# Two more batches turned by VectorE, and the stores of a cross-attention kernel put off

## The reference, cut to what matters

```python
rgb, geo = transpose(x), transpose(g)          # (16, 1024, 128)
def heads(x, w): return (x @ w.T).reshape(b, n, H, d).transpose(0, 2, 1, 3)
def xca(q, k, v):
    attn = softmax(einsum('bhni,bhnj->bhij', q, k) * scale, axis=-1)
    return merge_heads(einsum('bhnd,bhde->bhne', v, attn))
res_p2r = xca(heads(rgb, wq_rgb), heads(geo, wk_point), heads(geo, wv_point)) @ proj_p2r.T
res_r2p = xca(heads(geo, wq_point), heads(rgb, wk_rgb), heads(rgb, wv_rgb)) @ proj_r2p.T
return transpose(rgb + res_p2r) + transpose(geo + res_r2p)
```

## Time and profile before

| | |
|---|---|
| median of 3 runs | 129.18 us (129.02 to 129.22) |
| the profiled execution's own time | 129.13 us |
| its span, first to last instruction | 127.1 us |
| busy: TensorE (PE), VectorE (DVE), ScalarE (ACT), GpSimd (POOL) | 120.8, 71.4, 86.4, 77.3 us |
| DMA moved | 34.25 MB, 25.69 MB read from HBM and 8.39 MB written |
| DMA queue of SP (q1), of ScalarE (q10) | 29.36 MB, 4.72 MB |
| the chain that ended last | PE 84%, DMA 5%, ACT 3% |

### The profile page before, as it was taken

One profiled execution on the slowest core, in us unless ns is written; L12 is line 12 of the kernel. 1 busy time (PEld: TensorE's weight loads), 2 busy tenths in 40 slices (PEclk: granted clock), 3 DMA queues, 4 the chain that ended last, 5 costly groups with the idle time before them and its releaser, 6 DMA issues.

```text
span 127.1 us, 2678 instructions
## 1 busy us (share of the span) xinstructions
PE 120.8 (95%) x858; PEld 110.0 (87%) x858; DVE 71.4 (56%) x210; ACT 86.4 (68%) x195; POOL 77.3 (61%) x41
## 2 busy tenths in 40 slices
PE   6979999999999999999999999999999998997990
PEld 6859998899898989898989989999989897985880
DVE  0035364637878625969653787862596965546210
ACT  4133967875959595878787595959587868588351
POOL 5000779685495958195958559595819595937700
PEclk9999999999999999999999999999999999999999
DMA  3999999999999999999999999999999750003435
GB/s 102 362 398 409 419 285 252 230 289 256 296 243 251 246 328 370 328 271 281 313 274 339 380 328 282 278 280 300 329 418 419 317 233 1 0 23 147 168 142 191
DMA packets 16493, 34.25 MB, mean 270 GB/s; under 512 B 1376, under 2 KB 9952, under 8 KB 16480
## 3 DMA queue, kind: packets, MB, share of 16 engines
q1 hardware_dynamic: 11840, 29.36, 72.9%
q10 hardware_dynamic: 4640, 4.72, 14.4%
HBM read 25.69 MB, written 8.39 MB: 268 GB/s over the span
## 4 chain that ended last, share of the span: by engine, by line
PE 84%; DMA 5%; ACT 3%; issue 2%; DVE 1%; SPq 1%; ACTq 1%
PE out_ps L312 32%; PE gram_bank L291 21%; PE sy_bank L342 6%; DMA g_raw<-in_ctx_dram 5%; PE gt_ps L270 5%; PE xt_ps L270 4%; PE t_bank L355 3%; PE sy_bank L366 3%; PE sy_bank L365 3%; PE t_bank L356 3%; ACT expd L454 2%; PE uv_bank L333 1%; PE uv_bank L335 1%; PE uv_bank L334 1%; DVE probs L568 1%
## 5 line engine op out<-in xcount | busy, mean ns | idle before, releaser
L205 POOL TENSOR_TENSOR x_lo<-x_raw,x_hi 128x1024 fp32r<-128x1024 f32 x16 | 38.0, 2378 | 39.0 <-ACT x_hi L425 39.0
L208 POOL TENSOR_TENSOR g_lo<-g_raw,g_hi 128x1024 fp32r<-128x1024 f32 x16 | 38.0, 2373 | 2.5 <-ACT g_hi L425 2.5
L291 PE MATMUL gram_bank<-gt,xt 128*128 128x128 f32 x256 | 33.8, 275 | 0.0
L291 PEld LDWEIGHTS gram_bank<-gt,xt 128*128 128x128 f32 x256 | 31.2, 192 | 0.0
L541 DVE COPY gt<-gt_ps 128x512 f32<-128x512 f32 x16 | 11.0, 687 | 18.9 <-PE gt_ps L270 18.9
L432 ACT COPY out_sb<-out_ps 128x512 f32<-128x512 f32 x31 | 18.0, 581 | 5.2 <-PE out_ps L312 3.9
L454 ACT ACTIVATE expd<-scores,min_neg 128x128 f32<-128x128 f32 x32 | 12.6, 396 | 8.6 <-DVE min_neg L551 8.6
L425 ACT CAST g_hi<-g_raw 128x1024 fp32r<-128x1024 f32 x16 | 16.9, 1055 | 0.0
L425 ACT CAST x_hi<-x_raw 128x1024 fp32r<-128x1024 f32 x16 | 16.6, 1037 | 0.0
L438 ACT COPY xt<-xt_ps 128x512 f32<-128x512 f32 x16 | 9.4, 586 | 9.1 <-PE xt_ps L270 9.1
L312 PE MATMUL out_ps<-x_hi,t_hi 128*128 128x512 f32 x31 | 13.6, 440 | 0.0
(11 more groups left out here) (80 smaller groups left out, 211.5 us busy)
## 6 DMA issues: line engine op xcount, KB each, us to landing
x_raw<-in_x_dram SPq DMA_DIRECT2D x15, 512.0 KB, 15.8
g_raw<-in_ctx_dram SPq DMA_DIRECT2D x15, 512.0 KB, 16.2
out_dram<-out_sb SPq DMA_DIRECT2D x15, 512.0 KB, 15.1
xz<-in_x_dram SPq DMA_DIRECT2D x8, 256.0 KB, 12.4
gz<-in_ctx_dram SPq DMA_DIRECT2D x8, 256.0 KB, 16.0
xz<-in_x_dram ACTq DMA_DIRECT2D x8, 256.0 KB, 11.8
gz<-in_ctx_dram ACTq DMA_DIRECT2D x8, 256.0 KB, 13.9
g_raw<-in_ctx_dram ACTq DMA_DIRECT2D x2, 256.0 KB, 4.6
```

What stands on the lines that cost most here:

```text
L205: nc.gpsimd.tensor_tensor(x_lo[:, slot, :], x_raw[:, raw_slot, :], x_hi[:, slot, :].bitcast(F32), ALU.subtract).then_inc(x_lo_ready, 1)
L208: nc.gpsimd.tensor_tensor(g_lo[:, slot, :], g_raw[:, raw_slot, :], g_hi[:, slot, :].bitcast(F32), ALU.subtract).then_inc(g_lo_ready, 1)
L291: last = nc.tensor.matmul(gram_ps, xt[:, b % 2, cols], gt[:, b % 2, cols], start=(t == 0), stop=(t == TILES - 1))
```

## The change

`VECTOR_GROUPS` replaces `VECTOR_PAIRS`. Its five pairs are (5, 6), (7, 8), (10, 11), (12, 13) and (14, 15), so batches 7, 10 and 13 move from TensorE to VectorE and batch 9 moves from VectorE to TensorE: ten on VectorE, six on TensorE (0 to 4 and 9). `issued_in` follows from it: the x loads of the five pairs stand at i = 2, 4, 7, 9 and 12, their g loads one step later, and the pairs are turned from steps 5, 7, 10, 12 and 14 on. A store stands ten steps behind (`STORE_LAG`) in place of five, the loop ends at B, and stores 6 to 14 stand behind it, after the last load. `OUT_SLOTS` goes from 5 to 11. SP's order up to the last pair's g load is then: plain loads 0 to 14, five pairs, stores 0 to 2. The rest of the diff puts the new names in the same places.

```diff
--- before.py
+++ after.py
@@ -15,7 +15,8 @@
 QUAD = 32
 RAW_SLOTS = 6
 SPLIT_SLOTS = 3
-OUT_SLOTS = 5
+OUT_SLOTS = 11
+STORE_LAG = 10
 PAIRS = 2
 OFF_HEAD = -3.0e38
 WARM = 36
@@ -23,7 +24,7 @@
 WQR, WKR, WKP, WQP, PP, PR, WVP, WVR = range(8)
 
 
-VECTOR_PAIRS = ((5, 6), (8, 9), (11, 12), (14, 15))
+VECTOR_GROUPS = ((5, 6), (7, 8), (10, 11), (12, 13), (14, 15))
 
 
 def bass_cross_channel_attention(nc: bass.Bass, x, ctx, weights, out):
@@ -43,7 +44,7 @@
     HALF = N // 2
     TILES = N // TILE
     QUADS = P // QUAD
-    on_vector = [b for pair in VECTOR_PAIRS for b in pair]
+    on_vector = [b for group in VECTOR_GROUPS for b in group]
     on_tensor = [b for b in range(B) if b not in on_vector]
     assert C == P and HALF == BANK and B == 16 and on_tensor[0] == 0
 
@@ -152,16 +153,17 @@
 
         def load_turned(eng, src, dst, loaded, pair, quads):
 
-            first = VECTOR_PAIRS[pair][0]
+            first, count = VECTOR_GROUPS[pair][0], len(VECTOR_GROUPS[pair])
             for q in quads:
-                into = dst[q * QUAD:(q + 1) * QUAD, pair % PAIRS, :, :]
+                into = dst[q * QUAD:(q + 1) * QUAD, pair % PAIRS, 0:count, :]
                 eng.dma_start(into.rearrange("p e (a m) -> p (e a) m", a=QUADS),
-                              src[q][:, QUADS * first:QUADS * (first + 2), :]).then_inc(loaded[pair % PAIRS], 16)
+                              src[q][:, QUADS * first:QUADS * (first + count), :]).then_inc(loaded[pair % PAIRS], 16)
 
         def pair_turned(eng, pair):
 
-            eng.wait_ge(xt_turned, 4 * pair + 4)
-            eng.wait_ge(gt_ready, 2 * VECTOR_PAIRS[pair][1] + 2)
+            last = VECTOR_GROUPS[pair][-1]
+            eng.wait_ge(xt_turned, 2 * on_vector.index(last) + 2)
+            eng.wait_ge(gt_ready, 2 * last + 2)
 
         def x_turned_half(eng, b, half):
 
@@ -171,8 +173,8 @@
                 eng.wait_ge(xt_copied, 2 * on_tensor.index(b) + 1 + half)
 
 
-        issued_in = {2 + 2 * pair if pair < PAIRS else VECTOR_PAIRS[pair - PAIRS][1] + 1: pair
-                     for pair in range(len(VECTOR_PAIRS))}
+        issued_in = {2 + 2 * pair if pair < PAIRS else VECTOR_GROUPS[pair - PAIRS][-1] + 1: pair
+                     for pair in range(len(VECTOR_GROUPS))}
 
         first, second = slice(0, HALF), slice(HALF, N)
         third, fourth = slice(HALF, HALF + HALF // 2), slice(HALF + HALF // 2, N)
@@ -230,7 +232,8 @@
 
 
 
-            for i in range(2, B + 4):
+
+            for i in range(2, B):
                 for b in range(5, B):
                     if i == max(2, b - 1 if b in on_vector else b - 3):
                         if b >= RAW_SLOTS:
@@ -244,8 +247,10 @@
                     load_turned(sp, x_turn, xz, xz_loaded, x_pair, (0, 1))
                 if g_pair is not None:
                     load_turned(sp, g_turn, gz, gz_loaded, g_pair, (0, 1))
-                if i >= 5:
-                    store(i - 5)
+                if i >= STORE_LAG:
+                    store(i - STORE_LAG)
+            for b in range(B - STORE_LAG, B - 1):
+                store(b)
             last_slot = (B - 1) % OUT_SLOTS
             sp.wait_ge(half_copied, 2 * B - 1)
             sp.dma_start(out[B - 1][:, first], out_sb[:, last_slot, first]).then_inc(last_stored[0], 16)
@@ -524,8 +529,8 @@
         @block.vector
         def _(dve):
             def turn_half(b, half, src, loaded, dst, turned):
-                n = on_vector.index(b)
-                pair, at = n // 2, n % 2
+                pair = [b in group for group in VECTOR_GROUPS].index(True)
+                at = VECTOR_GROUPS[pair].index(b)
                 dve.wait_ge(loaded[pair % PAIRS], 64 * (pair // PAIRS) + 64)
                 dve.wait_ge(gram_done, b - 1)
                 blocks = src[:, pair % PAIRS, at, :].rearrange("p (a j i) -> p j a i", a=QUADS, i=QUAD)
```

## The result

The changed kernel takes 136.28 us in the median of four runs, the kernel before 129.20 us. The ratio is 1.052, with a 95% interval of 1.045 to 1.060: 5% slower. Three of the runs took 135.25, 135.85 and 136.71 us; the profile is of the first, with a span of 133.2 us. The fourth took 170.5 us at a mean granted clock of 0.66, far from every other run here, and is left out of the ratio; without it the median is 135.85 us.

What follows compares the result with a forecast made beforehand. PE taken as the bound, with DMA a second bound of the same height, only 1.3 us ahead. 129.13 - 3.5 (PE's saving) + 9.5 (stall in step 14) + 1.0 (clock) = 136.1 us; range 131.3 to 139.6.

Steps and rivals of the forecast that it cites:

- the clock: PE's granted clock after the breaks in step 14: might fall to half speed, 0 to +4.6 us, taken as +1.
- the stall: Step 14: PE idle 9.5 us because the fifth pair's g lands at 101.3 us, wanted by 91.8.
- the short stall: Rival: less extra cost of mixing, landing near 97, stall 5 us, clock unhurt, 130.5 us; chance 0.09 (under 131.5, not faster).
- The place: Step 14: VectorE waits for the fifth pair's `xz` and `gz`, leaving PE idle ahead of y and t products.
- PE's saving: Steps 7, 10 and 13 lose 1.76 us each, step 9 gains it: 3.5 us less PE work.
- Pair four: Batches 12 and 13, wanted in step 12: g lands at 80.6 us, 0.6 us late.
- pair two: Batches 7 and 8, wanted in step 7: g lands at 46.9 us, 0.8 us late.
- The covered costs: 2.8 us more VectorE work, ScalarE's four extra issues, eleven output buffers and late stores: nothing, late stores 1 us at most.
- The cause that I gave: DMA: turned loads are slow as they move in 1 KB runs, 234 GB/s against 417 for 4 KB rows.
- The prices: DMA time ahead of the last g load: plain batch 2.5 us, store 1.28, two turned batches 9.0 to 10.6.

Runs made afterwards that it cites:

- the second trace: The changed kernel run once more, unedited, on another chip beside the kernel with filling matmuls on the zero tile; 133.97 us in the median (130.1 to 137.2).
- the kernel with plain load 14 behind: Changed kernel with SP's plain load of batch 14 issued behind the last pair's g transfers in place of ahead of them; 132.4 us (130.3 to 133.3).

## Why the prediction was right, point by point

- **The time**: 136.1 predicted, 136.3 measured. Against the profiled execution of 129.13: -3.5 + 9.5 + 1.0 = 7.0 were predicted; the profiled execution after is 6.1 longer. In it the parts are -3.4 (step 14's beginning), +7.3 (t product at 101.05 in place of 97.19 - 3.4 = 93.8), +1.6 (the clock), +0.3 (t product to the end of the scores in 2.05 us after a wait at full clock, 1.78 in the earlier trace rows) and +0.3 at the very end. So the stall was 2.2 us too long in the sum and the clock 0.6 too cheap.
- **That the number hit within 0.2 us was luck.** On another chip the same kernel took 130.1, 130.9, 137.0 and 137.2 us. Two of the seven executions that count thus lie under 131.5 us, in what I gave to the short stall with a chance of 0.09, and only 1% above the kernel before; the median there is 134.0. The place of the stall doesn't hang on this, the size of the loss does.
- **PE's saving** was as counted, and it was made in full. It shows in nothing, as the wait for the last g stands behind it. That this landing has nothing to do with PE's pace isn't shown: SP itself waited 6.0 us in all for pairs to be turned (three times, 2.3 at most).
- **The place** was right: `xz` and `gz` of the fifth pair, in two pieces, holding up the y and then the t product of step 14. Landings: x near 95 predicted, 92.8 measured; g 101.3 and 99.35. Pair four was 0.9 us late for VectorE (0.6 predicted), pair two wasn't (0.8 predicted; g at 45.1).
- **The covered costs** were covered: ten batches of VectorE work cost nothing (steps 7, 8, 10 and 11 last 6.28 us), and neither did eleven buffers and the late stores (129.28 us with the stores alone).
- **The cause that I gave was wrong.** "Turned loads are dear" was right and read from a rate; "because their runs are 1 KB" was my addition. 4 KB rows moved as slowly, and 1 KB runs to spread partitions moved at some 370 GB/s. The sum didn't use the cause, only the rate, so it survived. What would have failed is any advice drawn from it.
- **The prices don't add up as I added them.** Put off in the kernel before, five stores gave 0.56 us each in landing; put back in the changed one, 0.8 each in time (3.8/5), and neither is a clean price, as said above. In the sum, one plain load, two turned batches and three stores fewer made 8.0 us; the landing moved by 99.35 - 93.3 = 6.05. With 1.28 us a store that leaves 7.35 us for two turned batches, 3.7 each, less than the 4.5 of the stretch in which nearly only they moved. With 0.56 us a store on both sides a turned batch would be (46.5 - 15.1 - 3.4)/4.5 = 6.2 us and the landing 106.6, further off than my 101.3. So what one transfer costs depends on what moves beside it, and the landing came out within 2 us without its terms being confirmed one by one. Why a store should be cheap beside a turned load was not tried; that it reads SBUF and writes HBM while the loads do the reverse fits, and is only argued.
- **The clock**: +1.0 taken within 0 to 4.6, and 1.6 measured (2.7 in the second trace). The value by the rule of the Trainium skill (TensorE: Matmul & The Clock Gate, What's actually happening), nearer 2, was the better one. I leaned on the row that I had, a break of 0.7 us, and that row was far from the case.

## What to carry to other kernels

When an engine is busy to the last and no DMA wait is in the list of waits, compare for each load when it landed and when it was taken: a slack of 1.3 us with 9s in the DMA line is a second bound. Price an edit that trades engine work for transfers in DMA time along the queue's order, with a rate measured beside like traffic, and expect an error of some 2 us from it. Run a kernel that waits for DMA on more than one chip before believing its median. And ask of a slow transfer which partitions it writes before blaming its row length; here the same bytes to every fourth partition moved at 370 in place of some 270 GB/s.

## What I hadn't expected of the hardware

- From 20 to 24 us, where nearly only turned loads move, 4 KB rows to 32 neighbouring partitions ran at 213 GB/s, 1 KB runs to the same partitions at 235 and 1 KB runs to every fourth partition at 378, where 128-partition loads run at 417.
- PE's clock was at half after a break of only 2.0 us ahead of the y product, in the changed kernel, and stayed full over breaks of 2.0 and 2.0 us in the kernel with plain load 14 behind (t product at 99.15, next last product 2.05 us later). So a break of one length can leave the clock up or bring it to half. The 1.6 us of above were paid after the second break, of 3.4 us.
- In stretches where both DMA queues had work they shared packet for packet, not byte for byte: 316 packets of ScalarE's queue against 331 of SP's were 0.30 against 1.14 MB.
- A kernel whose end hangs on a DMA landing spreads over 130.1 to 137.2 us on one chip, where the kernel before, with 1.3 us of slack, stays within 128.9 to 130.3.
